# Adding and norming all expert rows ahead of the key and value products, with ScalarE and Pool taking the first choice's rows of 20 tiles

## The reference

```python
xn = _layernorm(x)
x = x + _L0_gnn_ref(xn, edge_attr_64, ...) + _L0_mix_ref(xn[None], ...)[0]
x = x + _L0_ffn_ref(_layernorm(x)[None], ...)[0]      # 8 experts, the best 2 of each node
xn = _layernorm(x)
x = x + _L1_gnn_ref(xn, src, dst, edge_weight, ...) + _L1_mix_ref(xn[None], ...)[0]
x = x + _L1_ffn_ref(_layernorm(x)[None], ...)[0]      # 16 experts, the best 2 of each node
```

## Time and profile before

| | us |
|---|---|
| time, median of 3 runs | 2177.92 (2177.54 to 2179.30) |
| the profiled execution: its own time | 2177.88 |
| its span, first to last instruction | 2175.8 |
| the stage `keys_and_values` in it | about 1134.9 to 1288.3 |
| mean granted clock of TensorE, of full speed | 0.915 |

### The profile page before, as it was taken

The page is one execution under the profiler, slowest core; times in us unless marked ns, Lnnn a source line. Parts: engine busy times, 40 slices in busy tenths (PEclk is TensorE's granted clock), DMA queues, the critical chain, the costliest instruction groups (busy, mean ns, idle before and its releaser), DMA issues. The chain is left out here.

```text
span 2175.8 us, 35585 instructions
## 1 busy us (share of the span) xinstructions
PE 1802.7 (83%) x10583; PEld 1413.6 (65%) x10584; DVE 1249.2 (57%) x3264; ACT 708.5 (33%) x1624; POOL 984.2 (45%) x1571
## 2 busy tenths in 40 slices
PE   7499689876485999999975999869999764999976
PEld 5266466554354999999962556546776642888865
DVE  6654796985565454444458657734454575333336
ACT  4222334443530121212127941123322231233324
POOL 0576786785111222222220547878877000455542
PEclk9999899988696999999986899979999886999998
DMA  7565554554641101011114324444444227122234
GB/s 237 153 155 139 151 143 122 148 139 109 252 182 46 37 29 37 30 36 33 33 48 138 97 61 158 114 124 112 137 123 122 86 90 320 56 65 63 65 80 133
DMA packets 171241, 239.50 MB, mean 110 GB/s; under 512 B 74145, under 2 KB 139261, under 8 KB 168692
## 3 DMA queue, kind: packets, MB, share of 16 engines
q0 software_dynamic: 42336, 112.74, 18.4%
q1 hardware_dynamic: 116884, 113.45, 16.1%
q10 hardware_dynamic: 11904, 11.96, 1.7%
HBM read 184.86 MB, written 56.12 MB: 111 GB/s over the span
## 5 line engine op out<-in xcount | busy, mean ns | idle before, releaser
L656 POOL DMA_INDIRECT agg_message<-table,edges_src x638 | 624.4, 979 | 177.7 <-POOL agg_rest L654 172.2
L2825 PEld LDWEIGHTS ex_p_h<-ex_xT,ex_own_up 128*128 128x128 f32 (+1 forms) x2464 | 281.3, 192 | 2.7 <-issue 1.4
L2825 PE MATMUL ex_p_h<-ex_xT,ex_own_up 128*128 128x128 f32 (+1 forms) x2464 | 282.0, 276 | 1.0 <-DVE ex_xT L2876 1.0
L2784 POOL DMA_INDIRECT ex_x<-moe_in,route_token_at x58 | 57.3, 987 | 311.8 <-PE ex_p_x L2815 242.3
L2880 DVE COPY ex_own_up<-moe_up 128x1280 f32 x114 | 100.5, 882 | 168.7 <-PE ex_p_h L2825 167.9
L654 POOL MEMSET agg_rest<- 128x1 f32 x638 | 75.6, 119 | 185.0 <-DMA table<-layer_XN 74.9
L715 PE MATMUL agg_partial<-agg_message,moe_up 128*64 128x321 f32 x638 | 113.7, 495 | 44.2 <-issue 22.0
L2950 POOL DMA_INDIRECT ex_x<-moe_in,route_token_at x66 | 64.3, 975 | 174.1 <-PE ex_p_x L2981 93.8
L2868 ACT ACTIVATE ex_gate_h<-ex_p_h 128x640 f32<-128x640 f32 x56 | 39.4, 704 | 315.3 <-PE ex_p_h L2825 315.3
L3021 ACT COPY ex_own_up<-moe_up 128x1024 f32 x66 | 68.9, 1046 | 209.9 <-PE ex_p_h L2994 169.4
L2994 PEld LDWEIGHTS ex_p_h<-ex_xT,ex_own_up 128*128 128x128 f32 x1024 | 119.3, 195 | 16.2 <-issue 14.9
(11 more groups left out here) (666 smaller groups left out, 3708.3 us busy)
## 6 DMA issues: line engine op xcount, KB each, us to landing
moe_up<-in_f_w SPq DMA_DIRECT2D x8, 1386.0 KB, 20.1
agg_message<-in_edge_rows SPq DMA_DIRECT2D x54, 192.0 KB, 3.9
agg_message<-table,edges_src POOLq DMA_INDIRECT x638
sums<-agg_span SPq DMA_DIRECT2D x107, 80.2 KB
moe_up<-in_f_w SPq DMA_DIRECT2D x4, 2048.0 KB, 14.7
moe_down<-in_f_w SPq DMA_DIRECT2D x4, 2048.0 KB, 31.5
sums<-agg_span SPq DMA_DIRECT2D x107, 64.0 KB
moe0b_down<-in_f_w SPq DMA_DIRECT2D x8, 768.0 KB, 9.3
```

What stands on the lines that cost most here:

```text
L656: pool.indirect_dma_start(out=to[:, k * w:k * w + D], out_offset=None, in_=self.table, in_offset=bass.IndirectOffsetOnAxis(ap=self.edges.s ...
L2825: return pe.matmul(to, own_up[:, o:o + n], xT[:, k * D + c * P:k * D + (c + 1) * P], start=(c == 0), stop=(c == 1))
```

## The change

- VectorE now does all adds, statistics, `spreads` and `scales` ahead of the loop, by groups; `split_weights` and the marks of the first head jobs and edge groups, which stood ahead of the adds, come after them. The parts are now tiles 0 to 4, 5 to 19 and 20 to 24.
- For groups 1 to 4 the first choice's rows are no longer added by VectorE: ScalarE scales them in place (`scale_half`, one operation a tile), Pool adds a whole group to `X` in one operation of 128x1280, and VectorE waits for it (`half_added`) before it adds the second choice's.
- ScalarE's order is: scale group 1, root and norm of part 0, scale groups 2, 3 and 4, root and norm of part 1, root and norm of part 2, then the loop, which has neither norms nor roots left.
- SP issues both halves of the loads of groups 3 and 4, ahead of all stores. Pool's additions stand ahead of its wait for the stores.

```diff
-    parts = ((0, GT), (GT, 16), (16, NT))
-    adding = {i: range(2 * GT + 3 * i, 2 * GT + 3 * i + 3) for i in range(5)}
-    scaling = {1: 1, 4: 2}
-    norming = {2: (5, 9), 3: (9, 13), 4: (13, 16), 5: (16, 21), 6: (21, NT)}
+    parts = ((0, GT), (GT, 4 * GT), (4 * GT, NT))
+    measured = {0: 0, 3: 1, 4: 2}
...
             sp.wait_ge(cleared, 64)
-            for g in range(4):
+            for g in range(3):
                 load(sp, g, 0)
-            store(0)
-            load(sp, 4, 0)
-            for g in range(1, NG):
+            for g in range(3, NG):
+                for s in range(2):
+                    load(sp, g, s)
+            for g in range(NG):
                 store(g)
...
             head.number(pool)
+            for g in range(1, NG):
+                pool.wait_ge(half_scaled, g * GT)
+                x = X[:, g * GT * D:(g + 1) * GT * D]
+                pool.tensor_tensor(x, x, got[g % 3][:, 0:GT * D], ALU.add).then_inc(half_added, 1)
             pool.wait_ge(stored, NG * 16)
...
                     dve.wait_ge(loaded[g % 3], (g // 3 + 1) * 32)
+                if n == 0 and s and g:
+                    dve.wait_ge(half_added, g)
...
             c.did(dve.memset(heads[:, :], 0.0))
+            for g in range(NG):
+                if g == 0:
+                    for i in range(GT):
+                        add(i, 0)
+                    c.settle()
+                if g in (1, 4):
+                    scales(g // 4)
+                for i in range(g * GT, (g + 1) * GT):
+                    add(i, 1)
+                c.settle()
+                for i in range(g * GT, (g + 1) * GT):
+                    measure(i)
+                if g in measured:
+                    spreads(measured[g])
+            scales(2)
             head.split_weights(dve)
             for j in range(2):
                 head.mark(dve, j)
             for e in range(2):
                 edge_sums.mark(dve, e)
-            for g in range(2):
...
+            def scale_half(g):
+                act.wait_ge(loaded[g % 3], (g // 3 + 1) * 32)
+                for n in range(GT):
+                    half, i = got[g % 3][:, n * D:(n + 1) * D], g * GT + n
+                    act.activation(half, half, ACT.Copy, scale=routing.gate[0][:, i:i + 1]).then_inc(half_scaled, 1)
...
             load(act, 2, 1)
+            scale_half(1)
             roots(0)
             act.wait_ge(shift_ready, 1)
             norm(*parts[0])
-            load(act, 3, 1)
-            load(act, 4, 1)
+            for g in range(2, NG):
+                scale_half(g)
+            for n in (1, 2):
+                roots(n)
+                act.wait_ge(shift_ready, n + 1)
+                norm(*parts[n])
             act.wait_ge(head.split, 8)
```

More of the change, by code:

```diff
@@ L1549, in keys_and_values @@
             m.sem(n) for n in ("turned", "kept", "kv_made", "cut", "exped", "k_ready", "summed"))
+        half_scaled, half_added = m.sem("half_scaled"), m.sem("half_added")
         head = Head(nc, ctx, "head1", edge_sums.edges, counts, digits, low, joint, room)
@@ L1633, in step @@
                 k = i % 2
-                more_rows = adding.get(i, ())
                 dve.wait_ge(kv_made, i + 1)
@@ L1640, in step @@
                 c.did(tt(key[k][:, :], p_kv[k][:, 0:D], kb[:, 0:D], ALU.add))
-                for t in more_rows:
-                    add(t, 0)
                 c.settle()
                 ts(neg[k][:, :], key[k][:, :], 0.0, None, ALU.min).then_inc(cut, 1)
[L1645 to L1650, removed]
                 head.on_vector(dve, i)
@@ L1660, in step @@
                 phi.then_inc(k_ready, 1)
-                if i in scaling:
-                    spreads(scaling[i])
-                    scales(scaling[i])
             for k in range(2):
@@ L1729, in _ @@
                     keep(i + 1)
-                if i in norming:
-                    act.wait_ge(shift_ready, 2 if i < 5 else 3)
-                    norm(*norming[i])
                 act.wait_ge(cut, i + 1)
@@ L1738, in _ @@
                     edge_sums.move(act, e)
-                if i in scaling:
-                    roots(scaling[i])
         @block.tensor
```

## The result

The kernel after takes 2189.97 us (median of 5 runs, 2186.02 to 2190.96), the kernel before beside it 2178.25 (5 runs, 2177.54 to 2179.30): ratio 1.0049, interval 1.0037 to 1.0062. The profiled execution took 2189.97, with a span of 2188.2, 12.4 more than before's 2175.8. The forecast was 2191.4: slower by 13.5, measured 11.7.

What follows compares the result with a forecast made beforehand. VectorE is busiest in the start, then shares the pace with ScalarE, which alone is full later. `keep(0)` 11.5 us past break-even plus 2.0 for the clock gave +13.5: 2191.4 us, range 2181 to 2197.

Steps and rivals of the forecast that it cites:

- The loop gains 21.4: From `keep(0)` to step 8's Exp: 38.7 us instead of 60.1, without norms, four table loads and waits for VectorE.
- Pool holds VectorE: In the start, Pool's 2.91 us additions keep VectorE's two-input operations out: `spreads(0)` once, group 2's adds twice, 2.9 each.
- Rival 1: In the start, Pool's additions and VectorE's operations don't meet: `keep(0)` at 1181.3, 2183.4 us with the clock; chance 0.20.
- rival 4: Adds on Pool bring VectorE nothing: 8.3 us saved against 8.8 held or waiting; counted inside the forecast, no chance given.
- the rule of contention: GpSimd shares SBUF interfaces with VectorE and contends with its two-SBUF-input or 2-port instructions; without it, supposedly the second rival's sum.
- `keep(0)` at 1189.3: The copy that opens the product loop comes 11.5 us past break-even at 1177.8, because the start gets longer.
- Clock, +2.0: One early loop step with TensorE at 1.2 GHz, after a hole before step 2, costs 2.0 us; bounds 0 and 6.
- Rival 2: TensorE falls to 1.2 GHz in three or more first light loop steps: 2195.4 and up to 2198 us; chance 0.13.
- Rival 3, norms hidden: In the start, ScalarE's norms hide behind VectorE's work: `keep(0)` at 1172.5, 2172.6 us; chance 0.05.
- Later stages, 0: From step 8 on both kernels hold the same work, so lateness there stays to the end, with nothing added.
- The gathers' earlier start worth nothing: Pool's gathers start near 1193 instead of 1213, but the ring holds four groups and their first product stays in step 14.

Runs made afterwards that it cites:

- e4: Changed kernel with each of Pool's four group additions cut into five of 128x256, 20 operations in all; ratio 1.0034 to the kernel before.
- e6: Kernel before plus two 128x1280 Pool additions, and a memset, on data of their own that nobody needs; ratio 1.0025 to the kernel before.
- e1: Changed kernel with VectorE adding the first choice's rows of all tiles itself, no ScalarE scaling and no Pool additions; 2186.79 us.
- e3: Changed kernel with ScalarE still scaling, but VectorE instead of Pool adding each scaled group in one operation; ratio 1.0013 to the kernel before.
- e5: Changed kernel, VectorE adding scaled groups instead of Pool, split_weights, first two head jobs' marks and weighs moved early, last root amid the norms; 2179.25 us.
- e2: Changed kernel with split_weights and the first marks put back ahead of the adds; ratio 1.0036 to the kernel before.
- g2: Changed kernel with eight edge groups instead of four in this stage, their products from step 6 on; 2184.51 us.
- g1: Kernel before with six edge groups instead of four in this stage; 2175.96 us, ratio 0.9984.

## Why the prediction was right

The mechanism and most terms of the sum were right; that the total came out within 2 us is in part luck, as the fourth and the sixth point show.

- *The loop gains 21.4.* Measured 21.38; step 8's Exp came 38.71 after `keep(0)`, forecast 38.7. Step 0's Exp came 8.33 after it.
- *Pool holds VectorE.* Right at each of the three places: one small operation of `spreads(0)` at 2.86, adds of up to 3.10, and group 2 lost 7.30 - 2.06 = 5.2 where 2.9 twice was forecast. e4 and e6 show the mechanism apart from the semaphores. Rival 1, no meeting, is out; rival 4's "adds on Pool bring VectorE nothing" was too mild: the whole help costs 3.85 (e1), and Pool's part of it 5.4 (e3). One sentence on the rule of contention is a slip: without it the sum would be the first rival's, not the second's.
- *`keep(0)` at 1189.3.* Measured 1187.4, 1.9 early. Pool's first addition began 0.6 before the forecast moment, since a scaling took 0.42 (2.10 for five) and not 0.49, and `spreads(0)` ended 0.4 earlier; tiles 5 to 19 had their variance at 1174.45, not 1175.9, as the two holds of group 2 came to 5.2 and not 5.8 and Pool's later moments followed the scalings; 15 norms took 7.47, not 7.7. Group 4's landing is 1155.5 + 7.7 = 1163.2 by the prediction's own terms, not 1162.8, and it was in by 1161.7; either moment puts Pool's addition into the same adds. The shape of the sum stands; its sizes were somewhat too large.
- *Clock, +2.0.* This term failed: it measured 0. A slow product did come, but in step 1 and not before step 2:

```profile
1194.63 3.62 PE L1762 MATMUL kv_p_kv<-layer_kw,layer_XNT 128*128 128x512 f32 x4 [2.35 <-ACT layer_XNT L1701]
...
1199.82 1.98 PE L1762 MATMUL kv_p_kv<-layer_kw,layer_XNT 128*128 128x512 f32 x4 [0.38 <-ACT layer_XNT L1701]
```

  The window of the slow one (columns as in the earlier trace rows) has the granted clock at 0.53, behind 2.35 us of idling; in the next 1.57 us it is 1.00.

```profile
1194.63:1198.25 3.62, 3.62 (x7) 1.38 (x8) 0.43 (x1) 3.61 (x8) 3.02 (x5) 0.53 0.37 111
```

  The 3.62 us against 1.98 lie beside ScalarE's table load, its Exp of step 0 and the `weigh` behind it (1194.60 to 1199.5), and the next Exps don't come late: steps 0 and 1 are 3.78 apart. Until the stage's end the granted clock stays at 1.00. Rival 2 is out.
- *Rival 3, norms hidden.* Out: VectorE waited 2.85 us for `roots(2)` behind the 15 norms, as argued, and e5, which puts that root amid the norms, is part of what gains.
- *Later stages, 0.* The two errors in the stage (-1.9 and -2.0) would have put the kernel at +9.6, and the stage did grow by 9.45 and 9.64. The medians are 11.7 apart, and both profiles of the changed kernel have a rest 2.5 to 2.8 us longer. So the total came near the forecast partly by luck: what was charged too much in the stage came back behind it, where the forecast had nothing. From the first gather of `attend` to the last Pool's chain takes 390.7 us before, 393.7 and 393.1 after, with 2.9 to 3.0 of waiting for TensorE in each (the last window of the table above shows Pool busy for 313 of 408 us there); what grew is the time of Pool's own gathers (busy 309.1, 312.0 and 311.3). But it is 390.7 in e2 too, whose stage is as long as after's, and 393.6 in e3, whose stage is 5.4 shorter, and e2's and e4's rests are 0.9 and 1.2 *below* before's. So a tie to the later start isn't seen, and scatter is the likelier reading; with one profile of most kernels it isn't proven, and it stays open.
- *The gathers' earlier start worth nothing.* Right for this kernel (34.1 us of waiting for step 14). With more groups in the stage g2 gains some 5 us, of which g1 has 3.5 without the earlier start.

## What to carry to other kernels

Work given to Pool was not free for VectorE here: price it as up to the length of the Pool instruction on VectorE's own timeline, and compare with VectorE doing it itself (here 2.88 against 1.49 us). A phase that is pulled ahead of a loop must be filled on every engine: look for work of the loop's first steps that could run while the phase's loads are in flight. When a chain gets its data earlier, check that the next buffer down the line has room, or the gain is parked there (here Pool waited 34.1 us).

## What the runs showed of the hardware

- The hold ends with the Pool instruction that causes it (2.86 and 3.10 us with 2.88 us additions, 2.39 with e6's of 2.34 to 2.39, 0.94 with additions of a fifth of the size).
- It is not confined to operations with two tensor inputs: 128x64 float32 operations with one were held for up to 2389 ns (e6). My expectation of e6 left this out, though a cast in the earlier trace rows had shown it. Statistics were not held (and 1.73 for five in e4). The Trainium skill (SBUF — State Buffer, "Who interferes with whom") has a rule for both: one port pair is shared, taken by one of the two engines for a whole instruction, and VectorE needs it for two SBUF inputs or in a 2-port mode. The runs agree on the whole instruction, e4 above all, and on operations with two inputs; in which mode the marks and casts run no trace shows.
- Pool's addition of 128x1280 in five pieces cost 3.45 us against 2.88 in one.
